# Two light blocks of one tiled phase: double slots, a new schedule and a reordered last batch

## The reference

```
h  = modulate(layernorm(x))                       # per batch
light: xl = layernorm(h)*g+b; q,k,v = xl @ wqkv   # 8 heads of 64
       each window of 64 queries attends to its own and both neighbour windows (192 keys)
       light_out = softmax(q k^T / 8) v @ wo_l
heavy: 256 query rows and 256 key rows chosen by two router scores
       full softmax over the 256 keys, @ wo_h, put back at the rows chosen
x2 = x + gate_a * (light_out + heavy_out)
z  = modulate(layernorm(x2))
y  = square(relu(z @ W_fc^T)) @ W_proj^T;  spikes of a 5 step neuron driven by y
out = x2 + gate_b * spikes / 5
```

## Time and profile before

| | us |
|---|---|
| median of 3 runs (lowest to highest) | 973.71 (972.23 to 974.93) |
| the profiled execution | 968.1 |
| its span, first to last instruction | 966.3 |
| PE busy, share of the span | 838.0 (87%) |
| ACT busy | 586.2 (61%) |
| DVE busy | 571.9 (59%) |
| POOL busy | 399.5 (41%) |
| mean granted clock of TensorE | 0.942 of full |

### The profile page before, as it was taken

The page is one execution under the profiler, slowest core; times in us unless marked ns, Lnnn a source line. Parts: engine busy times, 40 slices in busy tenths (PEclk is TensorE's granted clock), DMA queues, the critical chain, the costliest instruction groups (busy, mean ns, idle before and its releaser), DMA issues.

```text
span 966.3 us, 23395 instructions
## 1 busy us (share of the span) xinstructions
PE 838.0 (87%) x8914; PEld 640.2 (66%) x8914; DVE 571.9 (59%) x1602; ACT 586.2 (61%) x1682; POOL 399.5 (41%) x437
## 2 busy tenths in 40 slices
PE   5658789889988999899988999799988999899565
PEld 2435566677765876578766876578766876687365
DVE  6646644684657665774567664874567665625244
ACT  1156666576656766676566765676666765777232
POOL 3422031265623653275524553365525542251333
PEclk8889679999999999999999999989999999999768
DMA  9220012200130003200230012200220012100100
GB/s 317 76 82 1 13 45 72 61 2 12 40 110 29 2 34 94 61 2 13 74 81 23 1 40 88 62 2 13 73 82 24 2 40 61 56 2 2 44 18 23
DMA packets 32480, 45.33 MB, mean 47 GB/s; under 512 B 3929, under 2 KB 26721, under 8 KB 32369
## 3 DMA queue, kind: packets, MB, share of 16 engines
q1 hardware_dynamic: 26944, 31.24, 10.2%
q0 software_dynamic: 4608, 12.59, 3.9%
q10 hardware_dynamic: 816, 0.00, 0.0%
HBM read 28.85 MB, written 14.97 MB: 45 GB/s over the span
## 4 chain that ended last, share of the span: by engine, by line
PE 63%; DVE 19%; ACT 6%; issue 6%; DMA 2%; POOL 2%; SPq 0%; DVEq 0%; POOLq 0%; ACTq 0%
PE ps_unit L895 27%; PE ps_y L1006 9%; PE ps_unit L943 6%; PE ps_turned L1055 5%; PE ps_turned L1090 3%; PE ps_unit L948 3%; PE ps_turned L1075 3%; PE ps_scores L1038 3%; PE ps_scores L1029 2%; ACT probs L829 2%; DVE row_min L1307 2%; DVE hT L1343 1%; ACT hT L794 1%; DVE bn L1269 1%; DMA late<-in_L_wmod 1%
## 5 line engine op out<-in xcount | busy, mean ns | idle before, releaser
L829 ACT ACTIVATE probs<-ps_scores,row_min 128x192 f32<-128x192 f32 (+2 forms) x384 | 161.3, 425 | 116.4 <-DVE row_min L1307 79.0
L839 ACT ACTIVATE probs<-probs,row_inv 128x192 f32<-128x192 f32 (+2 forms) x384 | 155.6, 457 | 0.0
L1307 DVE TENSOR_REDUCE row_min<-ps_scores 128x2 f32<-128x512 f32 (+1 forms) x128 | 78.6, 614 | 97.5 <-PE ps_scores L1038 68.5
L895 PE MATMUL ps_unit<-xT,wfcT 128*128 128x512 f32 (+1 forms) x432 | 111.5, 400 | 6.8 <-DVE xT L1248 6.2
L895 PE MATMUL ps_unit<-xT,wqkv 128*128 128x512 f32 x384 | 109.7, 422 | 3.3 <-POOL xT L653 3.3
L1055 PEld LDWEIGHTS ps_turned<-ident,probs 64*128 64x128 f32 x1280 | 57.2, 142 | 77.8 <-issue 71.8
L1006 PEld LDWEIGHTS ps_y<-wprojT,hid_parts 128*128 128x128 f32 x768 | 100.0, 191 | 9.8 <-issue 6.0
L432 POOL TENSOR_TENSOR hid<-hid 128x512 f32<-128x512 f32 (+1 forms) x64 | 64.7, 1011 | 99.7 <-ACT hid L807 97.8
L1006 PE MATMUL ps_y<-wprojT,hid_parts 128*128 128x256 f32 x768 | 105.2, 285 | 0.2
L1055 PE MATMUL ps_turned<-ident,probs 64*128 64x64 f32 x1280 | 82.9, 241 | 22.9 <-DVE loT L1324 18.6
L895 PEld LDWEIGHTS ps_unit<-xT,wfcT 128*128 128x128 f32 x432 | 77.6, 204 | 31.3 <-issue 18.7
(11 more groups left out here) (158 smaller groups left out, 1679.6 us busy)
## 6 DMA issues: line engine op xcount, KB each, us to landing
xa<-in_L_attn_x SPq DMA_DIRECT2D x8, 512.0 KB, 5.1
routed<-sorted_rows SPq DMA_DIRECT2D x16, 256.0 KB, 3.1
lx<-in_L_attn_x SPq DMA_DIRECT2D x8, 512.0 KB, 3.8
out_x<-spikes SPq DMA_DIRECT2D x16, 256.0 KB, 3.2
routed_out<-late SPq DMA_DIRECT2D x8, 256.0 KB, 2.1
full<-mod_rows SPq DMA_DIRECT2D x7, 256.0 KB, 5.0
sorted_rows<-hn,rank POOLq DMA_INDIRECT x64, 2.4
gate_a<-mod_rows SPq DMA_DIRECT2D x8, 128.0 KB, 3.5
```

Source lines behind the costliest of these rows:

```text
L829: ins = act.activation(probs[:, probs_buffer(s), probs_columns(s, part)], ps_scores[:, part, lo:hi], ACT.Exp, bias=row_min[:, s % 3, part: ...
L839: ins = act.activation(rows, rows, ACT.Identity, scale=row_inv[:, s % 3, part:part + 1])
L895: ins = pe.matmul(ps, w(wi, k, w_cols), a(ai, k, a_cols), start=(n == 0), stop=(n == 3 * KD - 1))
L1307: ins = dve.tensor_reduce(row_min[:, s % 3, :], ps_scores[:, :, lo:hi], AX.X, ALU.min)
```

## The change

`SPAN = 2`: a light slot now holds two neighbouring blocks of 128 queries of one pair of heads, so that an iteration has 8 light and 8 heavy slots. The scores of the two blocks stand side by side in the two score banks (384 of 512 columns each), the output of the second block in the last 128 columns of the same score banks, that of the first where it was. The heavy slots are as before. Because the second output lies in the score banks, `attend(n)` of a light slot waits for the exponentials of slot `n + 3`, and a new copy, `copy_spread`, stands before the minimum on DVE. All units and row stages are dealt out anew over 16 slots, DVE's row stages are cut in halves and stand between units, LO 3 goes to slot 1 of the next iteration, and the last iteration has a list of its own, with the heavy slots ahead of the last four light ones (`LAST_ORDER`) and the heavy output projection (HX), its store and its gather inside it. In the tail only LX 2 and LX 3 (the light output projections of the last two blocks) are left ahead of the MLP. `raw_wproj[0]` is loaded later, into `hid`, as its own buffer is gone.

```diff
+SPAN = 2
-LIGHT = PAIRS * T
+LIGHT = PAIRS * T // SPAN
 SLOT_UNITS = {
...
+    0: [("Q", 2), ("HT", 0), "stats1a", "stats1b", ("K", 2), ("HT", 1)],
+    1: [("Q", 3), ("HO", 1), ("HO", 0), "center_a", "center_b", ("LO", 3), "modulate", ("K", 3)],
+    2: [("V", 3), ("HV", 1)],
+    3: [("HV", 0), ("HQ", 0), "add", "stats3a", "stats3b", ("HK", 0), "norm3"],
+    4: [("Z3", 0), ("Z3", 1), "stats2", ("FC", 0), "router0", ("FC", 1)],
+    5: [("YA", 0), ("SR", 0), ("FC", 2), "router1", "compare0a", ("YA", 1), "compare0b", ("FC", 3)],
+    6: [("FC", 4), ("YA", 2), ("RK", 0), ("SR", 1), "norm2", ("FC", 5), ("YA", 3)],
+    7: [("FC", 6), ("YA", 4), "compare1a", ("YA", 5), ("FC", 7)],
+    8: ["compare1b", ("HK", 1), ("HQ", 1)],
+    9: [("YA", 6), ("RK", 1)],
+    10: [("ZT", 0), ("ZT", 1), ("YA", 7)],
+    11: ["y01", ("NK", 0), ("NV", 0), ("NQ", 0), "y02", "y03"],
+    12: [("LO", 0), "y04", "y05", "y11"],
+    13: [("LO", 1), "y12", ("NK", 1), "y13"],
+    14: ["y14", ("LO", 2), ("NQ", 1), "y15", ("NV", 1)],
+    15: [("NV", 2)],
 }
+LAST_ORDER = [*range(LIGHT // 2), *range(LIGHT, SLOTS)] + [p * T // SPAN + m for m in range(T // SPAN) for p in (2, 3)]
+LAST_UNITS = {
+    0: [("HT", 0), ("HQ", 0), ("HT", 1), ("HK", 0)],
+    1: [("HO", 0), ("V", 3), ("HO", 1), ("LO", 3)],
+    2: [("HV", 0), ("HV", 1), ("HQ", 1)],
+    3: [("HK", 1), "add", "stats3a", "stats3b", "norm3"],
+    4: [("Z3", 0), ("Z3", 1)],
+    5: [("FC", 0), ("Q", 2)],
...
+    12: [("FC", 6), ("YA", 4), ("FC", 7), ("YA", 5)],
+    13: [("HX", 0), ("HX", 1), ("YA", 6), ("YA", 7)],
+    14: ["y01", "y02", "y03", "y04", "y05"],
+    15: [("LX", 0), ("LX", 1), "y11", "y12", "y13", "y14", "y15"],
+}
+POOL_SLOTS = {"rstd1": 0, "gather": 2, "rstd3": 3, "rstd2": 4, "norm_rows": 4, "scatter0": 8, "scatter1": 12}
+LAST_POOL_SLOTS = {"gather": 1, "rstd3": 3, "tail_gather": 13}
+FIRST_UNITS = {4: [("WF", 0), ("WF", 1)], 5: [("WF", 2), ("WF", 3), ("WP", 0)], 6: [("WP", 1), ("WP", 2), ("WP", 3)]}
...
+        ps_oT = [t[:, :, 6 * W:6 * W + P] for t in (ps_turned, ps_scores)]
...
             def exp_step(n, s):
-                for part in range(2):
+                for w, k in slot_parts(s):
...
             def scores(segment, b, n, s):
-                    for h, c in ((0, 0), (1, 1), (1, 0), (0, 1)):
+                    for k in range(SPAN):
+                        for h, c in ((0, 0), (1, 1), (1, 0), (0, 1)):
...
+                            ins = pe.matmul(ps_scores[c * W:(c + 1) * W, w, score_columns(s, w, k)],
...
             def turn(n, s):
-                for i in range(3 if s < LIGHT else 4):
+                for i in range(SPAN * 3 if s < LIGHT else 4):
...
             def attend(segment, b, n, s):
+                if s < LIGHT:
+                    pe.wait_ge(spread_copied, spread_count(n))
+                    pe.wait_ge(exp_ready, min(n + 4, SLOTS * B))
...
+                    for k in range(SPAN):
...
+                            ins = pe.matmul(ps_oT[k][halves[h], g ^ k * h, :], v[halves[g], m, cols[h]], both,
...
             def minimum(n, s):
+                for w in range(2):
+                    if key_columns(s, w, 0) == key_columns(s, w, 1):
+                        ins = dve.tensor_reduce(row_min[:, n % 3, w, :], ps_scores[:, w, 0:SPAN * 3 * W].rearrange(
+                            "p (k n) -> p k n", k=SPAN), AX.X, ALU.min)
+                    else:
+                        for k in range(SPAN):
...
+            def copy_spread(n, s):
+                if s >= LIGHT:
+                    return
+                p, m = light_slot(s)
+                dve.wait_ge(oT_ready, n + 1)
+                dve.wait_ge(scores_ready, min(n + 5, SLOTS * B))
+                dve.tensor_reduce(loT[:, p, (m + 1) * P:(m + 2) * P], ps_oT[1].rearrange("p g n -> p n g"), AX.X,
+                                  ALU.add).then_inc(spread_copied, 1)
...
             def iteration(segment, b, first=False, last=False):
+                        invert(n + 1, slot_at(s + 1, last))
+                    if not (first and s < 2):
+                        copy_spread(n - 2, slot_at(s - 2, last))
                     if not (last and s + 2 >= SLOTS):
+                        minimum(n + 2, slot_at(s + 2, last))
...
             iteration("last", B - 1, last=True)
+            add_rows(B - 1, 0)
+            stats3(B - 1, 0)
+            third_norm(B - 1, 0)
+            for n in (SLOTS * B - 2, SLOTS * B - 1):
+                copy_spread(n, slot_at(n % SLOTS, True))
+                copy_out(n, slot_at(n % SLOTS, True))
+            unit("tail", B, ("LX", 2))
+            unit("tail", B, ("LX", 3))
+            add_rows(B - 1, 1)
+            stats3(B - 1, 1)
```

More of the change, by code:

```diff
@@ L92, with slot_work @@
 PROJECTED_AHEAD = [("NQ", 1), ("NK", 1), ("NV", 0), ("NV", 1), ("NV", 2)]
+def slot_work(slot, first, last):
+    if last:
+        return LAST_UNITS.get(slot, [])
+    work = [u for u in SLOT_UNITS[slot] if not (first and u in EARLIER_UNITS)]
+    return work + FIRST_UNITS.get(slot, []) if first else work
 def slot_units(slot, first, last):
-    units = [u for u in SLOT_UNITS[slot]
-             if not (first and u[0] in MLP_UNITS) and not (last and u[0] in NEXT_UNITS)]
-    return units + FIRST_UNITS.get(slot, []) if first else units
+    return [u for u in slot_work(slot, first, last) if isinstance(u, tuple)]
@@ L102, in iteration_units, with slot_at @@
+def slot_at(position, last):
+    return LAST_ORDER[position] if last and 0 <= position < SLOTS else position % SLOTS
 def iteration_units(first, last):
@@ L712, in _ @@
             iteration("last", B - 1, last=True)
-            gather(B - 1, True, in_tail=True)
-            for half in range(2):
-                rstd3(B - 1, half)
+            rstd3(B - 1, 0)
+            add_x("tail", B, ("LX", 2))
+            add_x("tail", B, ("LX", 3))
+            rstd3(B - 1, 1)
             for u in SEGMENTS["tail"]:
-                unit("tail", B, u)
+                if u[0] != "LX":
+                    unit("tail", B, u)
             final(pool, B - 1, 0)
@@ L1156, in drain, with stats1 @@
                 return ps_unit[bank], drained[bank]
-            def stats1(n):
-                dve.wait_ge(x_loaded, 16 * n + 16)
-                for t in range(T):
+            def stats1(n, tiles=range(T)):
+                if tiles.start == 0:
+                    dve.wait_ge(x_loaded, 16 * n + 16)
+                for t in tiles:
                     ins = dve.bn_stats(bn6[:, 0, t, :], xa[:, t, :])
+                if tiles.stop < T:
+                    return
                 ins.then_inc(ln_chain, 1)
@@ new lines, in row_stage @@
+            def row_stage(segment, b, name, first):
+                if name == "add" and not first:
+                    add_rows(b - 1)
+                elif name in ("stats3a", "stats3b") and not first:
+                    stats3(b - 1, tiles=TILE_HALVES[name[-1]])
+                elif name == "norm3" and not first:
+                    third_norm(b - 1)
+                elif name[0] == "y" and not first:
+                    neuron(b, int(name[1]), int(name[2]))
+                elif name in ("stats1a", "stats1b"):
+                    stats1(b + 1, TILE_HALVES[name[-1]])
+                elif name in ("center_a", "center_b"):
+                    center(b + 1, TILE_HALVES[name[-1]])
+                elif name == "modulate":
+                    modulate(b + 1)
+                elif name == "stats2":
+                    stats2(b + 1)
+                elif name in ("router0", "router1"):
+                    router_scores(b + 1, int(name[-1]))
+                elif name in ("compare0a", "compare0b", "compare1a", "compare1b"):
+                    compare(segment, b + 1, int(name[7]), TILE_HALVES[name[-1]])
+                elif name == "norm2":
+                    second_norm(b + 1)
```

421 lines of the change are left out of this document (206 added, 215 removed).

## The result

The changed kernel takes 1029.1 us (median of 4 runs, 1018.7 to 1032.0), the kernel before 973.0 in the same comparison: ratio 1.056, 95% interval 1.048 to 1.064. Forecast were 970.0 and a range of 942 to 990. Repeated in two later sets of runs it took 983.0 us against 967.4, ratio 1.016 (1.013 to 1.020), and 1023.6 against 974.5, ratio 1.051 (1.047 to 1.055). It is slower in each, but 41 to 46 us come and go with something that the kernel doesn't set; the kernel before moves with it, by 6 to 7 us between these sets.

The account below looks back on a forecast made before the run. TensorE's own work was taken as the bound, 99.4 of 107.85 us per loop iteration. 966.3 - 7.8 (first iteration) + 2.1 (loop) + 2.0 (last and tail) = 962.6, with 1.8 and 5.6 added 970.0; range 942 to 990.

Parts of the forecast that it names:

- Merged phase: Light slots: a double phase of transposes, attend and scores takes 1.97 us for 2.30; with drains, 3.2 us saved per iteration.
- Waits of the new loop: Each loop iteration: 13.0 us of waits including 1.65 for the clock, on 95.2 of work, giving 108.2 for 107.85.
- B: Rival, chance 0.29: chains overlap better and half the gap is filled; loop iteration 103.9, time 944 us.
- C: Rival, chance 0.20: the attend waits for exponentials, 0.4 in seven slots; loop iteration 111, time 988 us.
- E: Rival, chance 0.04: the clock stays at its lower level through slot 5; 5 us more per iteration, time 1000.
- 0.75 + 0.05 + 0.42 + 1.0 + 1.65 = 3.9: Light slots: the chain from scores through exponentials ends before TensorE's units and transposes, so the attend waits nothing.
- The term of 5.6 us: Added to the profiled span: the median of runs is 973.71 for 968.1 profiled, taking 964.4 to 970.0.
- First iteration: Before the loop: eight pairs fewer shorten it from 163.3 to 155.5 us, -7.8 (bounds -13 and +2).
- Last iteration and tail: From the last iteration's start: 118.4 for 117.1 us, +0.75 for the clock, so +2.0 (bounds -10 and +8).
- I count 34.9 from HX to the first FC matmul: Tail: the stretch from the heavy output projection to the last MLP takes 34.9 us, for 20.7 now.
- Clock: Loop, slot 4: after a wait of 6.9 us two FC units run at the lower level, costing 1.65 us net.
- faster: Whole kernel: chance 0.50 of being faster by more than 0.3%, 0.21 from the forecast's own range and 0.29 from B.

Follow-up runs that it names:

- r_after: The changed kernel run again unchanged in a later set, without late signals: 983.0 us, ratio 1.016 to the kernel before.
- e2: Changed kernel with the loop's four indirect gather loads replaced by four plain loads of as many bytes: 989.6 us, ratio 1.013 to the kernel before.
- e1: Changed kernel with the loop's gather waiting until V 3 is drained: 1011.6 us, ratio 1.036 to the kernel before.
- v2_a: Changed kernel with early loop slots and last iteration reordered, gather behind scores 4, tail copies ahead of the addition: 961.8 us, ratio 0.984.
- v3: v2_a with five small edits: three ScalarE drains, half the statistics and some units moved earlier: 949.4 us, ratio 0.982 to the kernel before.

## Why the prediction was wrong, point by point

- **Merged phase: right in the sum, with luck in the terms.** The earlier trace rows has one block's 1.15. TensorE's rows of a double one:

```profile
443.94 0.58 PE L1132 MATMUL ps_turned<-ident,probs 64*128 64x64 f32 x12
444.46 0.45 PE L1157 MATMUL ps_turned<-probsT,v 64*64 64x128 f32 x8
...
445.18 0.81 PE L1106 MATMUL ps_scores<-kT,qT 64*64 64x192 f32 x14
445.93 1.67 PE L1082 MATMUL ps_y<-wprojT,hid_parts 128*128 128x256 f32 x12
```

  The first scores matmul starts at 445.06. So transposes, attend and scores take 0.52, 0.60 and 0.87, 1.99 us in all, where 0.51, 0.71 and 0.75, 1.97 in all, were forecast: the attend's miss and the scores' cancel.
- **Waits of the new loop: right where the signals come on time.** In r_after the waits of one iteration are 11.4 us (K2 1.3, HO 0.6, Z3 2.3, FC 4.0, YA2 0.6, NK0 2.3, scores 0.3), forecast 11.35 without the clock; FC is 1.1 below its term and NK0 0.65 above. TensorE's busy time in it is 97.6, where 95.2 and 1.65 for the clock were forecast, 0.7 too little. This iteration takes 109.0; the mean of the loop is 109.85 for 108.2. The attend's wait for exponentials is nothing there, as put. B, C and E never came, though behind the late signals one attend does wait 0.7 to 0.9 for exponentials.
- **The step that failed: the 0.05 us from the scores' end to the spread copy in "0.75 + 0.05 + 0.42 + 1.0 + 1.65 = 3.9", by which slot 2 ("3.95 + 0.5") was to have no wait.** I took each release at the end of its row. From scores 4's last row to the copy it was 3.3 us (413.56 to 416.89), in r_after 0.1 (392.84 to 392.95). With late signals slots 2 and 3 of the iteration at 392.6 take 9.6 and 8.9 us, in r_after 4.95 and 6.5, forecast 5.15 (3.95 + 0.5 and 0.7 for the attend) and 6.65; slot 1 takes 11.6 for 11.2, and the other slots agree within 0.2. Over the loop it is 117.06 for 109.85: 7.2 us, six times 43 of the 59 by which the time was missed. The comparison is of one kernel in two sets, so the amount is measured, and e2 shows that it takes the indirect loads; what differs between the sets, and whether it is the issue on GpSimd or the fetching of rows one by one, stays open. The earlier trace rows could not show it, since that trace is most likely of the kind without late signals.
- **The term of 5.6 us.** "The median of the runs is 973.71 for 968.1 profiled, 5.6 more" was taken for a difference between a profiled execution and others. For the changed kernel, profiled and median are 1029.7 and 1029.1, for r_after 981.6 and 983.0; the 5.6 is, by the marks above, most likely that between the two kinds of set.
- **First iteration: -7.8 forecast, -5.1 and -9.4 measured** (end 158.2 and 153.9 for 155.5). The two differ at a clock of 0.83 and 0.91, with no late signal in it. Kernels with the same first iteration end it anywhere from 153.7 (e1) to 159.0 (e2).
- **Last iteration and tail: the second step that failed.** +2.0 forecast, +11.5 and +10.7 measured, in both kinds of set. HX comes at 85.9 for 84; the miss is "I count 34.9 from HX to the first FC matmul": it is 43.3 and 43.0. That the last attend stands behind the third norm was forecast; it waits 8.4 there. TensorE's row of it:

```profile
976.97 0.70 PE L1157 MATMUL ps_turned<-probsT,v 64*64 64x128 f32 x8 [8.37 <-DVE loT L1433]
```

  With the copies ahead of the addition the stretch is 39.2 (v2_a) and 36.5 (v3), but other things differ in them too. Which term of the 34.9 was short stays open, as it was not written down by term.
- **Clock.** The gap of 4.9 us before FC 0 is followed by a granted clock of 0.53 from 438 to 444, as forecast, and around the gap of 4.0 us in r_after it is 0.50 from 410 to 416. The one at 420 to 426 is there only with the late signals; in r_after the stretch of the same slots is at 1.00.
- Without any late signal the forecast would still have been off, and the sign wrong. The span of r_after is 979.5 for 962.6: 9.9 more in the loop, 8.7 in the last iteration and tail, 1.6 less in the first. What I gave to "faster" leaned on B, for which no row spoke but the room in it.

## What to carry to other kernels

Before a transfer that GpSimd issues with indices is moved beside other work, look at what signals TensorE gives in its time, and keep chains that hang on such a signal out of it: the delay is in no row of the kernel that doesn't have it. When two experiments are compared, run them in one set with the unchanged kernel beside them, and trace that one in the set too; I built two theories on pairs that differed in the chip, and a third question on a trace of the kernel before from the other kind of set. And a merge that takes work from the bounding engine pays only if what is left is dealt out so that a chain across engines (here add, norm, Z3, FC) has enough of that engine's work beside it: in one set the merged form was 1.6 per cent slower than the kernel before in one order and 1.8 per cent faster in another (v3, where three drains on ScalarE are earlier as well).
